# The first three batches' key DMAs: issued by GpSimd instead of SyncE

## The chip, the core and the metric

The kernel runs on one core of a Trainium2 chip. A core has TensorE (PE in the profile: matrix products into PSUM), VectorE (DVE), ScalarE (ACT), GpSimd (POOL) and SyncE (SP), which share a memory of 128 partitions and meet each other through semaphores. Each engine takes its own list of instructions in order. Transfers are asked for by an engine ("issued") and carried out by 16 DMA engines that the queues share; a semaphore is raised when a transfer has landed. The metric is the device time of one execution in microseconds.

## The reference

For 32 batches of 128 tokens by 128 features the reference chains four layers, each behind a layer norm and with a residual: cross attention A (16 heads of 8), a small mixture of experts, cross attention B (16 heads of 8, with an additive bias), and a large gated product of 8 heads by 8 experts (called C in the kernel).

```python
x = x + _L0_xattn_ref(_layernorm(x), ctx_1024, ctx_1024, mask_BxS2_if1, ...)   # A
x = x + _L0_ffn_ref(_layernorm(x), Ws1, Ws2, W1, W2, Wr)
x = x + _L1_xattn_ref(_layernorm(x), ctx_1024, mask_Bx1xSxS2_ff0, wq, wk, wv, wo)   # B
x = x + _L1_ffn_ref(_layernorm(x), q_w, k_w, v_w, o_w, sel_v_w, sel_o_w, route_scale)   # C

# inside A: keys, scores, and two masks (causal, and one row of 128 per batch)
scores = jnp.einsum('bhqd,bhkd->bhqk', q, k) * scale
full_mask = causal[None, None] & (mask[:, None, None, :] > 0)
scores = jnp.where(full_mask, scores, -jnp.inf)
p = jax.nn.softmax(scores, axis=-1)
```

## The kernel before, in words

One batch is worked on whole, in the stages A (with its experts), B and C, and the batches are pipelined: while C of one batch runs, B of a later and A of a still later one are interleaved with it. There is no scheduler. For each engine a list is written out by hand: `start()` for the prologue (batches 0 to about 6, some 145 us), `period(i)` for the middle and `end()`. Each call in a list, such as `a_queries(1)`, waits for its semaphores and then does its step for that batch; everything behind it on the same engine waits too.

TensorE computes the scores of A for four heads at once. For this the keys stand in a block-diagonal tile, `bdA`: each group of 32 partitions holds the keys of one head group and zeros elsewhere. The projected keys (`Kc0`, in the profile `Kc`) lie compactly, so they are spread into `bdA` by four small DMAs (8 partitions by 4 by 128 bf16, 8 KB each). A fifth DMA puts the mask row `keyrow` into `bdA`, and four more spread the queries `Qc0` into `Qb`. A's scores of a batch (`a_scores(b, 0)` on TensorE) need all nine. There is one `bdA`, one `keyrow` and one `Kc0`, reused by every batch, so:

- the spreading of batch b waits until the second scores of batch b-1 are done (`a_s2`);
- GpSimd makes the next `keyrow` (`a_masks` on GpSimd, from the raw mask `mrow_i`) only when the transfer of the last one has landed (`s_kmA`);
- ScalarE writes the next `Kc0` only when the last one's spreading has landed (`s_bdA`);
- SyncE loads the next raw mask (`masks(b)`) only when GpSimd has made the `keyrow` before it (`a_mask`).

SyncE issues nearly every DMA, in the order of its own list: inputs, masks, biases, A's spreading, and for B the writing of keys to DRAM rows (`k_rows`), their reading back into `bdB`, and the queries' spreading `Qs`. Its `masks(3)` stands right ahead of `a_queries(1)`. ScalarE issues the 512 KB weight loads (`raw`) that ScalarE and VectorE cut into `Vh`, `Vl`, `Oh`, `Ol` during the prologue, in between the attention work. TensorE fills part of its idle time in the prologue with a fixed number of matmuls by the identity whose result nobody reads (`psC<-ident_b`).

In the profile every matmul that goes through the helper has line L327, every ScalarE activation L1373, every DMA that SyncE issues through `load` L3832; a DMA issue is shown on the engine's queue as SPq or ACTq.

Of the kernel before, what the change touches and what calls it, by code (L numbers as in the profile page):

```python
# [14 lines left out]
SLOT = 32  # L15
# [23 lines left out]
def along(ap2, n):  # L39
    return ap2.unsqueeze(2).to_broadcast([ap2.shape[0], ap2.shape[1], n])  # L40
# [14 lines left out]
def program(nc, x_in, ctx_in, mask_in, bias_in, Wq0, bq0, Wk0, bk0, Wv0, bv0, Wo0, bo0,  # L55
# [4 lines left out]
    NH, HD = wq1.shape[1], wq1.shape[2]  # L60
    NJ = P // SLOT
# [19 lines left out]
    with ExitStack() as ctx:  # L81
# [3 lines left out]
        def sems(names):  # L85
            return [ctx.enter_context(nc.semaphore(n)) for n in names.split()]
# [173 lines left out]
        s_in = sems("in0 in1")  # L260
        s_bias = sems("bias0 bias1")
        s_out = sems("out0 out1")
        s_mask, s_bdA, s_qA, s_kmA, s_bdB, s_qB, s_rows, s_noK = sems("mask bdA qA kmA bdB qB k_rows no_K")
        s_bk, s_bq, s_wk0, s_wq0, s_wv0, s_wo0, s_attn1, s_ffn0, s_switch, s_rs, s_qk = sems(
            "w_bk w_bq w_wk0 w_wq0 w_wv0 w_wo0 w_attn1 w_ffn0 w_switch w_rs w_qk")
        s_raw = sems("w_raw0 w_raw1")
# [19 lines left out]

        IDENT, MINUS_HALF, ONEHOT, HIDDEN, LATE_B, SLOTS1, EARLIER = 4, 5, 11, 16, 19, 20, 28

        NG, NS = 12, 7

        place = {}

# [20 lines left out]
        def _(eng):  # L313
# [70 lines left out]
            def a_scores(b, t):  # L384
                if b not in BATCHES:
                    return
                if t == 0:
                    pe.wait_ge(s_const, LATE_B)
                    pe.wait_ge(s_kmA, 16 * (b + 1))
                    pe.wait_ge(s_qA, 16 * NJ * (b + 1))  # L390
                    pe.wait_ge(a_qb, b + 1)
                    pe.wait_ge(a_x2, b)
                elif t == 1:
                    pe.wait_ge(a_vb, b + 1)
                    pe.wait_ge(a_hT, b)
                else:
                    pe.wait_ge(a_nm, 4 * b + t - 1)
                o = heads_of(psA[:, t % 2, :])
                pe.wait_ge(s_bdA, 64 * (b + 1))
                mm(o, Qb[:, t, :], bdA[:, t], True, False)  # L400
                mm(o[:, :, LATE:], ident_b[:], over_heads(late_b[:], NJ), False, True).then_inc(a_s, 1)

# [963 lines left out]
        def _(eng):  # L1366
# [67 lines left out]
            def a_keys(b):  # L1434
                if b not in BATCHES:
                    return
                act.wait_ge(a_k, b + 1)
                act.wait_ge(s_bdA, 64 * b)
                copy(Kc0[:], psA[:, 1, 0:P]).then_inc(a_kb, 1)

            def a_values(b):
# [1842 lines left out]
        def _(eng):  # L3284
# [84 lines left out]
            def a_masks(b):  # L3369
                if b not in BATCHES:  # L3370
                    return
                pool.wait_ge(s_mask, 16 * (b + 1))
                pool.wait_ge(s_kmA, 16 * b)
                G.tensor_scalar(keyrow[:], mrow_i[:], 0, MASKED, ALU.is_le, ALU.mult).then_inc(a_mask, 1)

            def a_keys(b):
                if b not in BATCHES:
                    return
                pool.wait_ge(a_kb, b + 1)
                pool.wait_ge(s_bkC, 1)  # L3380
                G.tensor_tensor(Kc0[:].unsqueeze(1), Kc0[:].unsqueeze(1), along(bkC[:], P), ALU.add).then_inc(a_ks, 1)

            def a_values(b):
                if b not in BATCHES:
# [76 lines left out]
            def start():  # L3461
                constants()
                a_root(0)
                a_keys(0)
                a_values(0)
                a_queries(0)
                a_masks(0)
                a_masks(1)
                more_constants()
                a_causal(0, 0)  # L3470
                a_causal(0, 1)
                a_causal(0, 2)
                a_causal(0, 3)
                a_root(1)
                zeros()
                a_keys(1)
                a_values(1)
                a_root2(0)
                a_queries(1)
                a_masks(2)  # L3480
                b_root(0)
                a_root(2)
                b_below(0, 2)
                b_below(0, 3)
                a_causal(1, 0)
                a_causal(1, 1)
                a_causal(1, 2)
                a_causal(1, 3)
                a_keys(2)
                a_root2(1)  # L3490
                a_values(2)
                a_queries(2)
                b_root(1)
                c_root(0)
                a_masks(3)
                b_below(1, 2)
                a_causal(2, 0)
                a_causal(2, 1)
                a_causal(2, 2)
                a_causal(2, 3)  # L3500
                b_below(1, 3)
                a_root(3)
                a_keys(3)
                a_root2(2)
                a_values(3)
                a_queries(3)
                c_root(1)
                b_root(2)
                c_gates(0, 0)
                c_gates(0, 1)  # L3510
                c_gates(0, 2)
                a_causal(3, 0)
                a_causal(3, 1)
                b_below(2, 2)
                b_below(2, 3)
                values(0, 0, 0)
                a_causal(3, 2)
                a_causal(3, 3)
                values(0, 0, 1)
                values(0, 1, 0)  # L3520
                values(0, 1, 1)
                a_root(4)
                values(0, 2, 0)
                values(0, 2, 1)
                values(0, 3, 0)
                values(0, 3, 1)
                a_masks(4)
                a_keys(4)
                values(0, 4, 0)
                values(0, 4, 1)  # L3530
                values(0, 5, 0)
                values(0, 5, 1)
                a_root2(3)
                a_values(4)
                values(0, 6, 0)
                a_queries(4)
                values(0, 6, 1)
                values(0, 7, 0)
                values(0, 7, 1)
# [288 lines left out]
        def _(eng):  # L3828
# [65 lines left out]


            def a_masks(b):
                if b not in BATCHES:
                    return
                sp.wait_ge(s_zero, 8)
                sp.wait_ge(a_mask, b + 1)  # L3900
                sp.wait_ge(a_s2, 4 * b)
                load(bdA[KROW:KROW + 1].rearrange("p t j s -> p (t j) s"), keyrow[:], s_kmA)
# [15 lines left out]
                load(bias_sb[:, b % 2], bias_in[b, 0], s_bias[b % 2])  # L3918

            def a_keys(b):  # L3920
                if b not in BATCHES:
                    return
                sp.wait_ge(s_zero, 8)
                sp.wait_ge(a_ks, b + 1)
                sp.wait_ge(a_s2, 4 * b)
                for j in range(NJ):
                    load(bdA[SLOT * j + ROW0:SLOT * j + ROW0 + HD, :, j, :], Kc0[SLOT * j:SLOT * (j + 1)], s_bdA)
# [40 lines left out]
            def start():  # L3968
                values0()
                out0()  # L3970
                weights_switch()
                loads1()
                inputs(0)
                keys0()
                queries0()
                masks(0)
                products2()
                products()
                inputs(1)
                a_queries(0)  # L3980
                a_keys(0)
                a_masks(0)
                masks(1)
                weights_ffn()
                b_keys(0, 0)
                masks(2)
                no_keys()
                a_masks(1)
                inputs(2)
                b_keys(0, 1)  # L3990
                bias(0)
                masks(3)
                a_queries(1)
                a_keys(1)
                bias(1)
                b_queries(0)
                a_masks(2)
                inputs(3)
                a_keys(2)
                b_keys(1, 0)  # L4000
                a_queries(2)
                b_keys(1, 1)
                b_queries(1)
                bias(2)
                bias(3)
                a_masks(3)
                inputs(4)
                a_keys(3)
                b_keys(2, 0)
                a_queries(3)  # L4010
                masks(4)
                b_keys(2, 1)
                b_queries(2)
                masks(5)
                a_keys(4)
                a_queries(4)
                a_masks(4)
                b_keys(3, 0)
                bias(4)
                b_keys(3, 1)  # L4020
                b_queries(3)
                inputs(5)
                a_masks(5)
                inputs(6)
                a_queries(5)
                b_keys(4, 0)
                masks(6)
                a_keys(5)
                store(0)
                b_keys(4, 1)  # L4030
                b_queries(4)
# [64 lines left out]
```

## Time and profile before

| | us |
|---|---|
| median of 3 runs | 1418.85 (1418.19 to 1422.15) |
| the profiled execution | 1420.08 |
| its span, first to last instruction | 1418.3 |
| PE busy | 1368.3 (96%) |
| DVE busy | 1284.7 (91%) |
| ACT busy | 1217.4 (86%) |
| POOL busy | 920.9 (65%) |

The busy share of an engine is a mean over the whole span. The prologue is another regime: in the first 3 of the page's 40 slices (35 us each) PE is busy for 6, 6 and 7 tenths, and from the fifth to the last but one for 9 tenths or more. DMA issues are not counted as busy. The chain of waits, followed back from the last instruction, is on PE for 85% of the span and on SyncE's queue (SPq) for 3%.

### The profile page before, as it was taken

The page shows a single profiled execution, that of the slowest core. Times are in us where ns is not written, and L with a number is a line of the kernel's source. Part 1 is how long each engine was busy: PE and PEld are TensorE (multiplying, and loading weights), DVE is VectorE, ACT ScalarE, POOL GpSimd, SP SyncE. Part 2 cuts the span into 40 slices and gives each one's busy share as a digit, 9 for nine tenths or more (in the row PEclk, how much of TensorE's full clock was granted, in tenths as well). Part 3 has the DMA queues.
Part 4 walks back from the last instruction along what each step waited for, and adds up shares of the span by engine and source line. Part 5 has one row for each costly group of instructions (what it writes and reads, how often), then busy time and mean ns, then how long its engine had stood idle before and what let it go on. Part 6 is the DMA issues. An engine that isn't in the chain of part 4 may idle for free.

```text
span 1418.3 us, 34471 instructions
## 1 busy us (share of the span) xinstructions
PE 1368.3 (96%) x9554; PEld 922.0 (65%) x9711; DVE 1284.7 (91%) x5266; ACT 1217.4 (86%) x4234; POOL 920.9 (65%) x1409
## 2 busy tenths in 40 slices
PE   6678999999999999999999999999999999999997
PEld 3356666666666666666666666666666676666664
DVE  3679999999999999999999999999999999999986
ACT  3568888899988889998888999888899988889886
POOL 3224666667667666766766676676667666766777
PEclk9999999999999999999999999999999999999999
DMA  5520001100111110011111001111100111100000
GB/s 140 163 78 23 27 28 30 30 17 17 28 29 30 30 29 13 20 28 29 30 29 29 16 18 28 29 29 30 28 15 19 29 29 29 30 22 11 20 3 5
DMA packets 99968, 44.98 MB, mean 32 GB/s; under 512 B 21249, under 2 KB 99777, under 8 KB 99777
## 3 DMA queue, kind: packets, MB, share of 16 engines
q1 hardware_dynamic: 82560, 34.13, 8.7%
q10 hardware_dynamic: 17216, 8.65, 2.1%
q8 instruction: 78, 1.28, 0.4%
q14 instruction: 114, 0.93, 0.2%
HBM read 25.70 MB, written 8.52 MB: 24 GB/s over the span
## 4 chain that ended last, share of the span: by engine, by line
PE 85%; DVE 4%; POOL 3%; SPq 3%; issue 2%; ACT 2%; DMA 1%; POOLq 0%; ACTq 0%; DVEq 0%
PE psC L327 58%; PE psA L327 12%; PE psB L327 6%; PE psB L555 3%; SPq L3832 2%; PE psC L637 2%; DVE PTB L2398 1%; POOL accO L3445 1%; PE psA L489 1%; DVE nmA L2273 1%; POOL TE L3433 1%; PE psA L442 1%; DVE TE L2531 1%; ACT PTB L1373 1%; POOL v_sb L3438 1%
## 5 line engine op out<-in xcount | busy, mean ns | idle before, releaser
L1373 ACT ACTIVATE TE<-psC,gateO 128x128 f32<-128x128 f32 x1024 | 289.0, 378 | 30.5 <-PE psC L327 27.3
L2531 DVE SCALAR_TENSOR_TENSOR TE<-psC,gateO,TE 128x128 f32<-128x128 f32 x1024 | 286.9, 343 | 21.6 <-PE psC L327 11.8
L1373 ACT ACTIVATE TE<-psC,gate 128x128 f32<-128x128 f32 x1024 | 298.2, 400 | 7.2 <-PE psC L327 1.8
L2531 DVE SCALAR_TENSOR_TENSOR TE<-psC,gate,TE 128x128 f32<-128x128 f32 x1024 | 284.0, 340 | 7.3 <-PE psC L327 2.6
L3445 POOL TENSOR_TENSOR accO<-accO,TE 128x512 f32<-128x512 f32 x192 | 246.5, 1284 | 53.8 <-DVE TE L2531 44.6
L327 PE MATMUL psC<-Oh,ch 128*128 128x512 f32 x512 | 269.0, 525 | 0.0
L327 PE MATMUL psC<-Vh,xTh 128*128 128x512 f32 x512 | 263.1, 514 | 0.9 <-ACT PS L1373 0.9
L3433 POOL TENSOR_TENSOR TE<-TE 128x256 f32<-128x256 f32 x256 | 189.6, 741 | 56.3 <-DVE TE L2531 41.3
L327 PE MATMUL psC<-Oh,cl 128*128 128x512 f32 x512 | 202.1, 395 | 0.0
L327 PE MATMUL psC<-Vh,xTl 128*128 128x512 f32 x512 | 201.7, 394 | 0.0
L327 PE MATMUL psC<-Ol,cb 128*128 128x512 bf16 x477 | 185.8, 390 | 0.0
L327 PE MATMUL psC<-Vl,xTb 128*128 128x512 bf16 x393 | 153.4, 390 | 0.0
L327 PEld LDWEIGHTS psC<-Ol,cb 128*128 128x128 bf16 x512 | 49.0, 96 | 141.1 <-issue 141.1
L327 PEld LDWEIGHTS psC<-Vl,xTb 128*128 128x128 bf16 x512 | 49.2, 96 | 139.2 <-issue 139.2
L3438 POOL TENSOR_TENSOR v_sb<-TE 128x128 f32<-128x128 f32 x256 | 118.7, 464 | 13.7
L2398 DVE CUSTOM_DVE_ANT_0 PTB<-psB,bias_sb 128x128 f32<-128x128 f32 x512 | 114.9, 285 | 8.8 <-PE psB L327 6.4
L3360 POOL TENSOR_TENSOR PTB<-nmB,PTB 128x512 f32<-128x512 f32 x64 | 67.1, 1049 | 83.6 <-DVE nmB L2398 83.5
L1373 ACT ACTIVATE PTA<-psA 128x512 f32<-128x512 f32 x160 | 90.0, 614 | 23.3 <-PE psA L489 13.8
L327 PEld LDWEIGHTS psC<-Vh,xTh 128*128 128x128 f32 x512 | 99.4, 194 | 13.1 <-issue 6.5
L327 PEld LDWEIGHTS psC<-Oh,ch 128*128 128x128 f32 x512 | 99.9, 195 | 10.3
L327 PEld LDWEIGHTS psC<-Oh,cl 128*128 128x128 f32 x512 | 97.8, 191 | 5.9
L327 PEld LDWEIGHTS psC<-Vh,xTl 128*128 128x128 f32 x512 | 97.8, 191 | 4.8
(233 smaller groups left out, 3399.8 us busy)
## 6 DMA issues: line engine op xcount, KB each, us to landing
bdB<-k_rows SPq DMA_DIRECT2D x128, 64.0 KB, 2.2
k_rows<-Kc SPq DMA_DIRECT2D x96, 64.0 KB, 2.0
Qs<-Qc SPq DMA_DIRECT2D x96, 64.0 KB, 1.9
raw<-in_L_ffn_v_w ACTq DMA_DIRECT2D x8, 512.0 KB, 4.2
raw<-in_L_ffn_o_w ACTq DMA_DIRECT2D x8, 512.0 KB, 4.0
x_sb<-in_x SPq DMA_DIRECT2D x32, 64.0 KB, 2.0
ctx_sb<-in_ctx SPq DMA_DIRECT2D x32, 64.0 KB, 2.0
Qb<-Qc SPq DMA_DIRECT2D x128, 8.0 KB
```

Of the source, the lines that this page charges most:

```text
L327: return T.matmul(o, l, r, start=start, stop=stop)
L442: m = T.transpose(psA[:, 1, r * P:(r + 1) * P], UA[:, r * P:(r + 1) * P], ident)
L555: m = T.transpose(psB[:, t % 2, j * P:(j + 1) * P], PTB[:, t, j, :], ident)
L637: m = T.transpose(ps[:, j * P:(j + 1) * P], PS[:, 4 * i + j], ident)
L1373: return A.activation(o, i, func, **kw)
L2398: m = V.tensor_tensor_reduce(PTB[:, t, j], psB[:, t % 2, j * P:(j + 1) * P], bias_sb[:, b % 2], -1.0, LEAST, ALU.add, ALU.min, nmB[:, t, j ...
L2531: m = V.scalar_tensor_tensor(TE[:, i, e], psC[:, p, e * P:(e + 1) * P], gates[:, e:e + 1], TE[:, i, e], ALU.mult, ALU.add)
L3360: G.tensor_tensor(PTB[:, t], along(nmB[:, t, :], P), PTB[:, t], ALU.subtract).then_inc(b_sub, 1)
L3433: G.tensor_tensor(TE[:, i, 0:2], TE[:, i, 0:2], TE[:, i, 2:4], ALU.add).then_inc(v_fe, 1)
L3438: G.tensor_tensor(v_sb[:, h], TE[:, i, 0], TE[:, i, 1], ALU.add).then_inc(v_fe, 1)
L3445: G.tensor_tensor(accO[:], TE[:, slot(b, H1)] if h == 1 else accO[:], TE[:, slot(b, H1 + h)], ALU.add).then_inc(o_fe, 1)
L3832: SY.dma_start(dst, src).then_inc(s, 16)
```

## The change

For batches 0, 1 and 2 the five DMAs that spread the keys and the mask row into `bdA` leave SyncE's list and enter GpSimd's, behind `a_masks(0)`, `a_queries(1)` and `a_queries(2)`. They have semaphores of their own (`s_bdA0`, `s_kmA0`), and everyone who waited for the old ones waits for the new ones up to the third batch. Keys and mask row are now issued together, the four key DMAs first. From batch 3 on SyncE issues as before. No computing instruction is added or taken away.

```diff
+        EARLY = 3
+        def keys_spread(n):
+            return (s_bdA0, 64 * n) if n <= EARLY else (s_bdA, 64 * (n - EARLY))
+        def key_masks(n):
+            return (s_kmA0, 16 * n) if n <= EARLY else (s_kmA, 16 * (n - EARLY))
...
@@ tensor: a_scores
-                    pe.wait_ge(s_kmA, 16 * (b + 1))
+                    pe.wait_ge(*key_masks(b + 1))
-                pe.wait_ge(s_bdA, 64 * (b + 1))
+                pe.wait_ge(*keys_spread(b + 1))
...
@@ gpsimd: a_masks
-                pool.wait_ge(s_kmA, 16 * b)
+                if b:
+                    pool.wait_ge(*key_masks(b))
...
@@ gpsimd
+            def a_spread(b):
+                pool.wait_ge(s_zero, 8)
+                pool.wait_ge(a_ks, b + 1)
+                pool.wait_ge(a_mask, b + 1)
+                pool.wait_ge(a_s2, 4 * b)
+                for j in range(NJ):
+                    G.dma_start(bdA[SLOT * j + ROW0:SLOT * j + ROW0 + HD, :, j, :],
+                                Kc0[SLOT * j:SLOT * (j + 1)]).then_inc(s_bdA0, 16)
+                G.dma_start(bdA[KROW:KROW + 1].rearrange("p t j s -> p (t j) s"), keyrow[:]).then_inc(s_kmA0, 16)
...
@@ gpsimd: start
                 a_masks(0)
+                a_spread(0)
                 a_masks(1)
...
                 a_queries(1)
+                a_spread(1)
                 a_masks(2)
                 b_root(0)
...
                 a_queries(2)
+                a_spread(2)
                 b_root(1)
...
@@ sync: a_masks, a_keys
-                if b not in BATCHES:
+                if b not in BATCHES or b < EARLY:
...
@@ sync: start (the calls for batches 0 to 2 are gone)
                 a_queries(0)
-                a_keys(0)
-                a_masks(0)
                 masks(1)
...
                 a_queries(1)
-                a_keys(1)
                 bias(1)
```

GpSimd's list before, from the queries of batch 1 to the stages of B and A behind them. `Qc` and `Kc` are the compact queries and keys, `rsB` and `rsA` the layer norms' roots.

```order
L3396 TENSOR_TENSOR Qc<-Qc,bqC 128x128 [waits a_qb]
L3374 TENSOR_SCALAR keyrow<-mrow_i 16x128 [waits kmA,mask]
L3335 TENSOR_TENSOR rsB<-rsB,minus_half 128x1 [waits b_ln]
L3335 TENSOR_TENSOR rsA<-rsA,minus_half 128x1 [waits a_ln]
L3360 TENSOR_TENSOR PTB<-nmB,PTB 128x512 [waits b_nm] x2
```

The same place in the changed kernel:

```order
L3416 TENSOR_TENSOR Qc<-Qc,bqC 128x128 [waits a_qb]
L3399 DMA bdA<-Kc 8x4x128 [waits a_s2,a_mask,a_ks]
L3399 DMA bdA<-Kc 8x4x128 x3
L3401 DMA bdA<-keyrow 1x16x128
L3384 TENSOR_SCALAR keyrow<-mrow_i 16x128 [waits kmA_pool,mask]
L3344 TENSOR_TENSOR rsB<-rsB,minus_half 128x1 [waits b_ln]
L3344 TENSOR_TENSOR rsA<-rsA,minus_half 128x1 [waits a_ln]
```

The five DMAs now stand between the queries and the next mask row, and that mask row waits (`kmA_pool`) for the fifth of them to land.

SyncE's list before, at the same time in the program: the raw mask of batch 3, the queries and keys of batch 1, then the bias and B's queries of batch 0.

```order
L3832 DMA bias_sb<-in_mask_Bx1xSxS_ff 128x128
L3832 DMA mrow_i<-in_mask_BxS_if 16x128 [waits a_mask]
L3832 DMA Qb<-Qc 8x4x128 [waits a_q2,a_s,a_qs]
L3832 DMA Qb<-Qc 8x4x128 x3
L3832 DMA bdA<-Kc 8x4x128 [waits a_ks]
L3832 DMA bdA<-Kc 8x4x128 x3
L3832 DMA bias_sb<-in_mask_Bx1xSxS_ff 128x128
L3832 DMA Qs<-Qc 32x4x128 [waits b_qh,const]
```

In the changed kernel:

```order
L3855 DMA bias_sb<-in_mask_Bx1xSxS_ff 128x128
L3855 DMA mrow_i<-in_mask_BxS_if 16x128 [waits a_mask]
L3855 DMA Qb<-Qc 8x4x128 [waits a_q2,a_s,a_qs]
L3855 DMA Qb<-Qc 8x4x128 x3
L3855 DMA bias_sb<-in_mask_Bx1xSxS_ff 128x128
L3855 DMA Qs<-Qc 32x4x128 [waits b_qh,const]
```

The keys are gone from this place. The raw mask with its wait for `a_mask` (the mask row that GpSimd makes) still stands ahead of the queries.

## Rows read from the trace of the kernel before

**Rows 1.** Busy by stretch: stretch, us; PE, PEld, DVE, ACT, POOL; PEclk, DMA, GB/s.

```profile
20.70:22.80 2.10, 0.01 (x1) 0.13 (x2) 0.00 (x0) 0.57 (x2) 0.00 (x0) 1.00 0.67 164
...
43.00:48.70 5.70, 4.82 (x26) 2.65 (x25) 3.80 (x12) 3.25 (x7) 0.78 (x2) 1.00 0.58 162
48.70:50.80 2.10, 0.02 (x1) 0.13 (x2) 0.91 (x3) 1.00 (x2) 0.46 (x1) 1.00 0.57 159
...
123.00:200.00 77.00, 76.16 (x534) 51.43 (x541) 71.18 (x290) 68.09 (x244) 51.73 (x80) 1.00 0.09 26
```

**Rows 2.** The chain of waits, 0 to 60 us: start, us, what.

```profile
19.25 3.30 DMA bdA<-keyrow
...
22.86 0.25 PE psA L327
...
41.95 0.65 POOL keyrow L3374
...
42.62 0.33 SPq L3832
...
48.14 2.31 DMA bdA<-Kc
...
50.80 0.25 PE psA L327
...
55.97 0.86 PE psC L327 x4
```

**Rows 3.** Timeline of GpSimd: start, us, engine line op out<-in [idle before <-releaser].

```profile
13.20 1.03 POOL L3374 TENSOR_SCALAR keyrow<-mrow_i 16x128 bf16<-16x128 int32 x1
...
41.24 0.63 POOL L3396 TENSOR_TENSOR Qc<-Qc,bqC 128x128 bf16<-128x128 bf16 x1 [1.65 <-ACT Qc L1373]
...
77.84 0.87 POOL L3396 TENSOR_TENSOR Qc<-Qc,bqC 128x128 bf16<-128x128 bf16 x1 [0.67 <-ACT Qc L1373]
84.37 0.55 POOL L3335 TENSOR_TENSOR rsB<-rsB,minus_half 128x1 f32<-128x1 f32 x1 [5.66 <-DVE rsB L2250]
```

**Rows 4.** Timeline of SyncE's DMA issues.

```profile
9.46 1.29 SPq L3832 DMA_DIRECT2D x_sb<-in_x  x1
...
43.06 2.89 SPq L3832 DMA_DIRECT2D Qb<-Qc  x4
45.99 2.81 SPq L3832 DMA_DIRECT2D bdA<-Kc  x4
...
76.25 2.92 SPq L3832 DMA_DIRECT2D bdA<-Kc  x4
...
81.61 2.91 SPq L3832 DMA_DIRECT2D Qb<-Qc  x4
```

**Rows 5.** All that touches bdA, 0 to 125 us: durations min/median/max in ns.

```profile
L3832 SPq DMA_DIRECT2D bdA<-Kc x16: 665/672/750, 16.4 to 106.6; - x16
...
L3832 SPq DMA_DIRECT2D bdA<-keyrow x4: 578/589/597, 19.2 to 96.5; - x4
...
DMA to landing us min/median/max: 1.7/3.1/4.1
```

**Rows 6.** Timeline of all engines: fillers, the clearing of bdA, two adds of one shape.

```profile
8.17 1.06 PE L327 MATMUL psC<-ident_b 128*128 128x512 bf16 x2
...
10.69 0.43 POOL L3389 TENSOR_TENSOR Vb<-Vb,bvb 128x128 bf16<-128x128 bf16 x1 [0.47 <-ACT Vb L1373]
...
13.41 0.69 DVE L2220 COPY bdA<-hides 128x2048 bf16<-128x2048 bf16 x1
...
16.02 4.70 PE L327 MATMUL psC<-ident_b 128*128 128x512 bf16 x21
...
35.16 0.23 DVE L2313 TENSOR_TENSOR ob<-obA,bob 128x128 bf16<-128x128 bf16 x1
```

**Rows 7.** The chain of waits, 56 to 90 us.

```profile
83.84 1.84 DMA Qb<-Qc
```

**Rows 8.** Who waited for whom in 0 to 125 us: us, times, longest.

```profile
ACT Vh L1373 <- DMA raw<-in_L_ffn_v_w: 7.8, 5, 2.7
```

More of the change, by code:

```diff
@@ L262, in program @@
         s_out = sems("out0 out1")
-        s_mask, s_bdA, s_qA, s_kmA, s_bdB, s_qB, s_rows, s_noK = sems("mask bdA qA kmA bdB qB k_rows no_K")
+        s_mask, s_bdA, s_qA, s_kmA, s_bdB, s_qB, s_rows, s_noK, s_bdA0, s_kmA0 = sems(
+            "mask bdA qA kmA bdB qB k_rows no_K bdA_pool kmA_pool")
         s_bk, s_bq, s_wk0, s_wq0, s_wv0, s_wo0, s_attn1, s_ffn0, s_switch, s_rs, s_qk = sems(
@@ L1437, in a_keys @@
                 act.wait_ge(a_k, b + 1)
-                act.wait_ge(s_bdA, 64 * b)
+                if b:
+                    act.wait_ge(*keys_spread(b))
                 copy(Kc0[:], psA[:, 1, 0:P]).then_inc(a_kb, 1)
@@ L3372, in a_masks @@
                 pool.wait_ge(s_mask, 16 * (b + 1))
-                pool.wait_ge(s_kmA, 16 * b)
+                if b:
+                    pool.wait_ge(*key_masks(b))
                 G.tensor_scalar(keyrow[:], mrow_i[:], 0, MASKED, ALU.is_le, ALU.mult).then_inc(a_mask, 1)
@@ L3920, in a_keys @@
             def a_keys(b):
-                if b not in BATCHES:
+                if b not in BATCHES or b < EARLY:
                     return
@@ L3987, in start @@
                 no_keys()
-                a_masks(1)
                 inputs(2)
@@ L3993, in start @@
                 a_queries(1)
-                a_keys(1)
                 bias(1)
                 b_queries(0)
-                a_masks(2)
                 inputs(3)
-                a_keys(2)
                 b_keys(1, 0)
```

## The prediction

> **What bounds the kernel now.** I read the busy time by stretch first. From 123 us on TensorE is busy 76.16 of 77 us [rows 1]: the middle is bound by TensorE, and this change adds and takes nothing there. So only the prologue can move, and what it gains or loses is handed on as one shift of everything behind it. The two stretches before the scores of batches 0 and 1 show TensorE idle for about 2.1 us each (0.01 and 0.02 us busy, [rows 1]). The chain of waits then names the last thing awaited. Batch 0: the mask row's DMA, issued at 19.25, landed 3.30 later, and the scores start at 22.86 [rows 2]. Batch 1: GpSimd's mask row at 41.95, SyncE's raw-mask load at 42.62, the eight issues from 43.06, the last key DMA at 48.14 landing 2.31 later, scores at 50.80 [rows 2, 4]. Batch 2: the last query DMA at 83.84, landing 1.84 later at 85.68 [rows 7]. So SyncE's queue does stand on the path in all three batches, and the question is what GpSimd's costs there.
>
> **The price of an issue on GpSimd.** No row shows one. SyncE needs 0.67 us for a key DMA and 0.59 for the mask row [rows 5]; the longest issue of SyncE that I see is 1.29 us [rows 4]. For an add of one shape (128x128 bf16) GpSimd takes 0.43 us and VectorE 0.23 [rows 6], so it is the slow engine for small work. I take 1.05 us, some 1.5 times SyncE's 0.70 spacing (2.81 over four, [rows 4]), nearer to the upper end since descriptors for 32 scattered pieces are small work of that kind. It is an estimate; the ends 0.59 and 1.29 go into the range. A lower price than SyncE's I exclude only by judgement. Five issues are 5.25 us (2.95 to 6.45). For the landing behind the end of an issue I take SyncE's: 3.30 - 0.59 = 2.71 in batch 0, 2.31 - 0.67 = 1.64 in batches 1 and 2 [rows 2, 5].
>
> The Trainium skill (DMA: Bandwidth & Descriptors, Specifications) gives about 1 us to the first byte for a DMA issued by GpSimd and 0.6 for one by SyncE. That would add 0.4 to each landing, and by its rule the sum below would be some 1.2 us higher (three landings). No run here shows it yet.
>
> **Batch 0.** GpSimd's mask row ends at 14.23 [rows 3], the clearing of bdA at 14.10 [rows 6], so the issues start at about 14.25, 2.1 us ahead of SyncE's (16.40). They end at 19.50, and the mask row lands at 22.21 instead of 22.55. Gain 0.34 us. By the quick end they land at 19.9, but then TensorE's 21 fillers, which end at 20.72 [rows 6], stand ahead of the scores: the gain stops at 2.1. By the slow end they land at 23.41: a loss of 0.86. The keys' and mask's departure from SyncE also pulls the raw mask of batch 1 and the expert weights 3.4 us ahead, of which nobody on the path has need.
>
> **Batch 1.** Here the change adds a loop that the trace of before lacks. GpSimd's queries end at 41.87 [rows 3] and the DMAs follow at 41.95. Behind them stands the mask row of batch 2, which waits for the fifth one's landing. Behind that mask row, on SyncE, stands the raw-mask load of batch 3 (it waits for a_mask), and behind this, on the same queue, the queries of batch 1. Before, mask row, raw mask and queries followed within 1.1 us (41.95 to 43.06). Now the mask row starts at 41.95 + 5.25 + 1.64 + 0.08 = 48.92, 6.97 late, and the queries' four DMAs go out from 50.03. The fourth starts 2.22 behind the first and lands 2.31 later, at 54.56, and with the same 0.35 to the start the scores begin at 54.9 instead of 50.80. The 2.86 us in which SyncE formerly issued the keys behind the queries are already taken off in this. Loss 4.1 us (quick end: 2.95 + 1.1 + 0.08 - 2.86 = 1.3, with the shortest landing, 1.7 from issue [rows 5]; slow end 5.3). Also GpSimd's roots for B and A, the first computing behind, come later, but B's transpose stands behind A's scores on TensorE and moves with them. What SyncE holds behind the queries (bias, B's query spreading) moves by the same.
>
> **Batch 2.** Queries end on GpSimd at 78.71 [rows 3], issues 78.79 to 84.04, landing 85.68, which is when the queries landed before. On SyncE four issues (76.25, 2.92 us, [rows 4]) go from ahead of k_rows, so the queries go out about 1.0 us earlier and stop being last. GpSimd is free at 84.04, ahead of B's root at 84.37 [rows 3]. Sum 0 (quick end -1.0, when the queries are last again; slow end +1.2).
>
> **TensorE's pace.** Its idle stretch ahead of batch 1's scores grows from 2.1 to about 6.2 us. The granted clock reads 1.00, the 2.4 GHz level, in every stretch [rows 1], yet the first fillers took 0.53 us each (8.17) and later ones 0.22 (16.02) [rows 6]: after idleness the engine works at less than half pace for a while. On the chain behind it 0.25 us of scores and 0.86 of fillers are TensorE's [rows 2]; at 2.4 times that they take 1.5 us more. I take 0.6, as if it came about in four of ten cases.
>
> **Sum.** -0.34 + 4.1 + 0 + 0.6 = +4.4 us on the profiled execution's 1420.08. That execution was 1.2 above the median of the runs; the shift does not depend on this, so the forecast is 1418.85 + 4.4 = 1423.2, 0.31% more. A change of 0.3% (4.3 us) is about what a measurement of this kernel can tell from none, so it lies at that border.
>
> **Rivals.**
>
> *GpSimd issues as fast as SyncE.* At 0.67 each (3.35), batch 0 gains the full 2.1, batch 1 loses 3.35 + 1.64 + 0.08 - 2.86 = 2.2, batch 2 gains 1.0: -0.9, time 1418. For it: the work per DMA is the same. Against: the adds above. With 0.59 each and landings of 1.1 it is -1.8, time 1417. The sign turns at about 0.8 us per issue; below that the kernel is not slower. Chance 0.24.
>
> *GpSimd's issues are held up.* VectorE is busy 3.80 of the 5.70 us in which they would go out for batch 1 [rows 1], with weight cutting. If each issue stretches to 1.29, it is 0.9 + 5.3 + 1.2 + 0.6 = +8.0, time 1427. For it: GpSimd's own small operations stretch in the busy stretches, the queries' add from 0.63 to 0.87 us and the mask row to 1.03 [rows 3]. Against: batch 0's issues fall where VectorE does little. Chance 0.22. The Trainium skill (SBUF — State Buffer, Who interferes with whom) says that GpSimd cannot write descriptors while VectorE runs an operation in a two-port mode, and that such a DMA took 3.1 us instead of 0.62; by its figure this rival would be the larger one. What stands in that stretch is mostly adds and subtractions of two inputs, which the page does not count among those modes.
>
> *The delay is absorbed.* ScalarE waits 7.8 us for weight loads in the prologue [rows 8]; if weights are what is late behind 51 us, a delay of A's scores costs only part. Of 4.1 about 3 would vanish, time 1420. Against: the weight cutting stands behind A's row maxima in VectorE's list and moves with them. Chance 0.10.
>
> *No loop, since the landing is seen early or the mask row is early enough.* That would need the landing wait not to bind; the wait list of the changed order names it, so I give it 0.04, at about 1417.
>
> **How the numbers follow.** The forecast has 0.40 and falls on both sides of the border, 0.27 above and 0.13 within. Rival one: 0.20 within, 0.04 faster. Rival two is slower, 0.22. Absorbed: within, 0.10. No loop: within 0.02, faster 0.02. So slower 0.49, same 0.45, faster 0.06. The range takes rival one's 1418 nearly whole and rival two's 1427: 1417.5 to 1427.5.
>
> **What would show it.** Five issues on POOLq at about 14.3, 42 and 79 us; their mean is the first test (1.05). The start of A's scores: 22.5, 54.6 and 90 or so (from 22.86, 50.80 and about 86). GpSimd's mask row of batch 2 at about 48.6, waiting for the DMA of the key row, then raw mask and queries on SyncE right behind. After 123 us all else shifted by one amount. I would be wrong if the issues take under 0.8 us, if SyncE's queries of batch 1 go out near 43, or if the shift at 123 us differs from that at batch 2's scores.

## Result

The changed kernel takes 1423.86 us (median of 14 runs), the one before 1420.32 in the same comparison; the ratio is 1.0025, 95% interval 1.0018 to 1.0032. That is 3.5 us slower where 4.4 were forecast (on a base of 1418.85, the median of the first three of these 14 runs of before).

The profiled execution alone would mislead. It took 1420.88, the fastest of the 14, and its span of 1419.1 is only 0.8 above the 1418.3 of before. Single executions of the unchanged kernel lie between 1417.4 and 1424.2 (94 of them, run beside the experiments). So the times below are ratios with their intervals, and the profiles are read for what follows what.

GpSimd's timeline in the changed kernel (start, us, engine line op), answering to [rows 3]:

```profile
14.55 2.44 POOL L3399 DMA_DIRECT2D bdA<-Kc  x4 [0.86 <-DVE bdA L2229]
16.98 0.53 POOL L3401 DMA_DIRECT2D bdA<-keyrow  x1
21.80 0.64 POOL L3384 TENSOR_SCALAR keyrow<-mrow_i 16x128 bf16<-16x128 int32 x1 [4.29 <-DMA bdA<-keyrow]
...
39.63 0.63 POOL L3416 TENSOR_TENSOR Qc<-Qc,bqC 128x128 bf16<-128x128 bf16 x1 [1.30 <-ACT Qc L1381]
40.25 2.30 POOL L3399 DMA_DIRECT2D bdA<-Kc  x4
42.54 0.53 POOL L3401 DMA_DIRECT2D bdA<-keyrow  x1
46.19 0.66 POOL L3384 TENSOR_SCALAR keyrow<-mrow_i 16x128 bf16<-16x128 int32 x1 [3.12 <-DMA bdA<-keyrow]
46.93 0.57 POOL L3344 TENSOR_TENSOR rsB<-rsB,minus_half 128x1 f32<-128x1 f32 x1
```

Batch 1's five DMAs are issued within 2.8 us (40.25 to 43.07), then the next mask row waits 3.12 us for the last of them to land. SyncE's issues, answering to [rows 4]:

```profile
46.88 0.33 SPq L3855 DMA_DIRECT2D mrow_i<-in_mask_BxS_if  x1
47.32 2.91 SPq L3855 DMA_DIRECT2D Qb<-Qc  x4
```

Raw mask and queries stand right behind that mask row, as the loop has it: 7.7 us from GpSimd's queries (39.63) to SyncE's (47.32), where before it took 1.8 [rows 3, 4]. TensorE (timeline), with the last fillers and the scores of batch 1:

```profile
45.00 2.11 PE L335 MATMUL psC<-ident_b 128*128 128x512 bf16 x9
52.81 0.35 PE L335 MATMUL psA<-late_b,ident_b 128*128 128x176 bf16 x1 [5.71 <-issue]
52.96 0.42 PE L531 MATMUL psB<-ident_r,xnB 128*128 128x128 f32 x1
```

It idles for 5.71 us instead of 2.1, and the first matmul that is recorded behind it takes 0.35 us instead of 0.24. The busy time by stretch (stretch, us; PE, PEld, DVE, ACT, POOL; PEclk, DMA, GB/s), answering to [rows 1], shows why:

```profile
50.00:52.80 2.80, 0.00 (x0) 0.14 (x2) 0.00 (x0) 0.00 (x0) 0.00 (x0) 0.90 0.62 181
52.80:54.00 1.20, 1.19 (x5) 0.70 (x5) 0.80 (x2) 0.28 (x1) 0.00 (x0) 0.50 0.00 0
54.00:55.00 1.00, 1.00 (x5) 0.66 (x6) 1.00 (x2) 0.28 (x1) 0.00 (x0) 0.50 0.00 0
```

The granted clock (PEclk) is 0.50, the 1.2 GHz level, for the first 2 us behind the idle stretch. In the kernel before it read 1.00 there.

What one DMA costs on either queue (durations min/median/max in ns), answering to [rows 5]:

```profile
L3399 POOL DMA_DIRECT2D bdA<-Kc x12: 547/548/807, 14.6 to 82.6; - x12
L3855 SPq DMA_DIRECT2D bdA<-Kc x4: 672/677/751, 106.2 to 108.4; - x4
L3401 POOL DMA_DIRECT2D bdA<-keyrow x3: 530/530/530, 17.0 to 83.1; - x3
```

GpSimd issues faster than SyncE, 0.55 against 0.67 us. The profile lists its DMAs as a queue of another kind (packets, MB, share of the 16 engines):

```profile
q0 software_dynamic: 480, 0.11, 0.0%
```

And who held SyncE's queue in the first 125 us (us, times, longest). Before, the mask row held it for 2.3 us in all, once:

```profile
SPq L3855 <- POOL keyrow L3384: 8.4, 2, 7.5
```

### The profile page after: what moved, and what is told of

It reads as the page before. It is cut to its first block, busy times and chain, and to the rows that moved or that the text cites. A ratio compares the mean times of both kernels' runs of the same rounds, so it can differ in the third digit from the quotient of the medians.

```text
span 1419.1 us, 34473 instructions
## 1 busy us (share of the span) xinstructions
PE 1370.1 (97%) x9554; PEld 922.9 (65%) x9711; DVE 1285.3 (91%) x5266; ACT 1219.2 (86%) x4234; POOL 930.6 (66%) x1424
## 4 chain that ended last, share of the span: by engine, by line
PE 87%; DVE 4%; POOL 3%; issue 2%; ACT 2%; SPq 1%; DMA 1%; POOLq 0%; ACTq 0%; DVEq 0%
PE psC L335 59%; PE psA L335 13%; PE psB L335 6%; PE psB L563 3%; PE psC L645 2%; DVE PTB L2407 1%; POOL accO L3465 1%; PE psA L497 1%; DVE nmA L2282 1%; POOL TE L3453 1%; PE psA L450 1%; SPq L3855 1%; DVE TE L2540 1%; ACT PTB L1381 1%; POOL v_sb L3458 1%
```

## The experiments

Each ratio is to the kernel before, run on the same chip in the same comparison (14 runs of the changed kernel, 6 of e1, 11 of each other); medians of different rows come from different comparisons, so rows are compared by their ratios. The fourth column is the time in us from GpSimd's queries of batch 1 (`Qc`) to the first matmul by `late_b` in batch 1's scores on TensorE, in the kernel's one profile: it leaves out what happened earlier in that execution. (The record of the matmul ahead of that one, `psA<-bdA,Qb`, is missing in most profiles, so this one serves as the mark.) The last is the mean over the runs of each run's mean granted clock.

| kernel | median us | ratio (95%) | Qc to scores | clock |
|---|---|---|---|---|
| before | 1420.53 (94 runs) | 1 | 9.56 | 0.9971 |
| changed | 1423.86 | 1.0025 (1.0018, 1.0032) | 13.18 | 0.9949 |
| e1 more fillers | 1423.34 | 1.0028 (1.0016, 1.0039) | 12.86 | 0.9972 |
| e2 queries first | 1419.33 | 0.9996 (0.9986, 1.0005) | 7.54 | 0.9960 |
| e3 mask row first | 1419.74 | 1.0000 (0.9990, 1.0009) | 9.37 | 0.9965 |
| e4 fewer fillers, before | 1420.97 | 1.0009 (1.0000, 1.0018) | 9.68 | 0.9954 |
| e5 roots first | 1420.59 | 1.0004 (0.9995, 1.0013) | 7.55 | 0.9958 |
| e6 batch 0 only | 1420.39 | 1.0000 (0.9991, 1.0009) | 9.58 | 0.9973 |
| e7 batch 1 only | 1422.80 | 1.0017 (1.0009, 1.0026) | 13.07 | 0.9963 |
| e8 queries first, before | 1421.18 | 1.0008 (0.9999, 1.0017) | 9.12 | 0.9965 |
| e9 two mask rows | 1420.52 | 0.9997 (0.9987, 1.0007) | 9.44 | 0.9970 |
| e10 batch 2 only | 1420.36 | 0.9994 (0.9985, 1.0003) | 9.74 | 0.9971 |
| e11 all three | 1419.37 | 0.9988 (0.9979, 0.9997) | 7.54 | 0.9976 |
| e12 fillers batch 0, before | 1421.36 | 1.0004 (0.9995, 1.0013) | 9.72 | 0.9970 |

**e1, more fillers.** Changed kernel, TensorE's list:

```diff
-                warm(9)
+                warm(29)
                 a_scores(1, 0)
```

> The changed kernel with 29 instead of 9 filler matmuls ahead of the scores of batch 1, so that TensorE's idle stretch there (5.71 us in the changed kernel's trace) shrinks to about 1.4. Pace theory (the idle stretch lowers TensorE's clock, and in most runs for longer than in the profiled one): the scores start at 52.8 as before, the granted clock reads 1.00 in 52.8 to 56, the mean clock of the runs returns from 0.994 to 0.999, and the time falls by 2 to 3 us, to about 1421. Loop theory alone (the late start is all there is, the clock costs nothing): the time stays at 1423.9 within 0.7.

Measured 1.0028. The timeline and the stretches:

```profile
47.61 6.42 PE L335 MATMUL psC<-ident_b 128*128 128x512 bf16 x29
55.10 0.24 PE L335 MATMUL psA<-late_b,ident_b 128*128 128x176 bf16 x1 [1.06 <-issue]
```

```profile
52.80:54.00 1.20, 1.20 (x6) 0.39 (x4) 0.00 (x0) 0.00 (x0) 0.00 (x0) 1.00 0.90 256
54.00:56.00 2.00, 0.86 (x6) 0.59 (x7) 0.63 (x2) 0.28 (x1) 0.00 (x0) 1.00 0.12 33
```

The idle stretch and the fall of the clock are gone (1.00 in both stretches, mean clock from 0.9949 to 0.9972), the time is not better. (In this execution batch 0's scores had started 1.0 us later than in the changed kernel's profile, and Qc was 2.6 later, so the absolute start says nothing; from Qc it is 12.86 against 13.18.) The pace theory (the idle stretch lowers TensorE's clock, and that is what costs) falls as an account of the loss: the clock did fall, and giving it back brought nothing that these runs can tell. By the two intervals taken together, a gain of up to some 2 us is not excluded.

**e4, fewer fillers.** The kernel before with `warm(9)` at this place taken out.

> The kernel before, without the 9 filler matmuls ahead of the scores of batch 1: nothing is later, but TensorE idles about 4.2 us there instead of 2.1. Pace theory: the granted clock falls below 1.00 at 50.8 to 53 in some or all runs, mean clock 0.995 to 0.997, time 1 to 3 us more than before. Loop theory alone: same time as before within 0.7 us.

Measured 1.0009 (1.0000 to 1.0018). The other side of e1, the stretches:

```profile
50.00:52.80 2.80, 1.93 (x7) 1.25 (x9) 1.54 (x3) 1.37 (x4) 0.00 (x0) 0.62 0.73 207
52.80:54.00 1.20, 1.20 (x4) 0.30 (x3) 1.20 (x4) 0.47 (x2) 0.00 (x0) 0.50 0.00 1
```

TensorE idles 4.14 us there, and the clock falls to the same level with nothing else changed. The one profile would not show that the longer idleness did it: in the profile of e12 the clock fell at the same place behind 2.25 us of idleness, about as long as in the kernel before, whose profile reads 1.00. What speaks for it is the mean clock, 0.9954 against 0.9968 of the kernel before in the same comparison. The version costs 0 to 2.6 us, 1.3 by the middle. So the price of a fall is at the edge of what these runs can tell, and e1 shows that it is not what made the changed kernel slow.

**e2, queries first.** Changed kernel, SyncE's list:

```diff
-                masks(3)
                 a_queries(1)
+                masks(3)
                 bias(1)
```

> The changed kernel with SyncE's raw-mask load of batch 3 moved behind the query DMAs of batch 1. Loop theory: the queries go out at 40.3 instead of 47.3, the scores then wait for the mask row (landing 46.1) and for the fillers (ending 47.1), and start at about 47.1 instead of 52.8; with the clock kept the time is 1423.9 - 5.7 - 2 = about 1416, under both kernels. Rival (GpSimd's slow landings are the price, whatever the order on SyncE): the scores start no earlier than 51 and the time stays at or above 1422.

Measured 0.9996, that is 4.1 us under the changed kernel by the ratios (4.5 by the medians): the loss is gone, with every GpSimd DMA still in place. GpSimd, SyncE and TensorE in its timelines:

```profile
40.03 0.63 POOL L3416 TENSOR_TENSOR Qc<-Qc,bqC 128x128 bf16<-128x128 bf16 x1 [1.39 <-ACT Qc L1381]
...
47.02 1.17 POOL L3384 TENSOR_SCALAR keyrow<-mrow_i 16x128 bf16<-16x128 int32 x1 [3.56 <-DMA bdA<-keyrow]
48.26 0.57 POOL L3344 TENSOR_TENSOR rsB<-rsB,minus_half 128x1 f32<-128x1 f32 x1
```

```profile
40.69 2.90 SPq L3855 DMA_DIRECT2D Qb<-Qc  x4
48.21 0.34 SPq L3855 DMA_DIRECT2D mrow_i<-in_mask_BxS_if  x1
```

```profile
47.57 0.24 PE L335 MATMUL psA<-late_b,ident_b 128*128 128x176 bf16 x1
49.27 0.33 PE L531 MATMUL psB<-ident_r,xnB 128*128 128x128 f32 x1 [1.46 <-DVE xnB L2262]
```

The queries go out at once and the scores start about as forecast (47.57 for 47.1), but the time falls by 4.1 to 4.5 and not by 7.7. From Qc the scores start 2.0 us earlier than in the kernel before, and the time is the same: B's transpose behind the first scores waits until 49.27 for batch 0's normalised input, whose root (48.26) stands behind the mask row on GpSimd. From Qc the transpose is at 9.24 us, where before it was at 9.64, so nearly all that the scores gained ends in the next wait.

**e5, roots first.** As e2, and on GpSimd:

```diff
                 a_spread(1)
-                a_masks(2)
                 b_root(0)
                 a_root(2)
+                a_masks(2)
```

> As the kernel with the queries first, and on GpSimd the roots of B (batch 0) and A (batch 2) now stand ahead of the next mask row, so that they do not wait for the landing of the mask row's DMA either. There the second matmul of the group waited until 49.27 us for B's normalised input. Loop theory (everything that stood behind the landing is what costs): root of B at about 46 instead of 48.2, B's transpose at about 47.8, all later work 1.5 us earlier than there: median 1417.5 to 1418, 2.5 to 3 under the kernel before. Rival (latency of GpSimd's DMAs itself, or the clock, decides now): 1419.3 as with the queries first.

Measured 1.0004; a miss. In its profile B's transpose starts 8.87 us behind Qc, against 9.24 in e2, a gain of 0.4 and not 1.5. GpSimd's root (48.39) waits for VectorE, which waits for the experts of batch 0 on TensorE, and behind the root a weight cut of 1.3 us on VectorE (48.93) still stands ahead of the normalised input (50.18); that chain is what is late next.

**e3, mask row first.** Changed kernel, GpSimd issues the mask row's DMA ahead of the four key DMAs.

```diff
+                G.dma_start(bdA[KROW:KROW + 1]..., keyrow[:]).then_inc(s_kmA0, 16)
                 for j in range(NJ):
                     G.dma_start(bdA[...], Kc0[...]).then_inc(s_bdA0, 16)
-                G.dma_start(bdA[KROW:KROW + 1]..., keyrow[:]).then_inc(s_kmA0, 16)
```

> The changed kernel with the mask row's DMA issued ahead of the four key DMAs on GpSimd. The loop then closes four issues (2.3 us) earlier. Loop theory: the next mask row on GpSimd starts at about 44 instead of 46.2, scores of batch 1 at 50.6 instead of 52.8, idle 3.5 us; time 1421.5, and if the clock does not fall at this idle length about 1419.5. Rival (the four key DMAs' landing decides, or landing counts from the last issue whatever the order): no change, 1423.9.

Measured 1.0000 (1419.74, next to the second of the two numbers, 1419.5). GpSimd and SyncE:

```profile
41.05 0.63 POOL L3398 DMA_DIRECT2D bdA<-keyrow  x1
41.67 2.18 POOL L3400 DMA_DIRECT2D bdA<-Kc  x4
43.94 0.89 POOL L3384 TENSOR_SCALAR keyrow<-mrow_i 16x128 bf16<-16x128 int32 x1
```

```profile
45.30 2.92 SPq L3855 DMA_DIRECT2D Qb<-Qc  x4
```

The landing now passes while the four key DMAs are issued, and the mask row waits for nothing: it starts 2.3 us behind the end of its DMA's issue, where it was 3.1. From Qc (40.47) the queries go out after 4.8 us instead of 7.7, and the loss is gone.

**e9, two mask rows.** Changed kernel, both orders as they are:

```diff
-        keyrow = sb("keyrow", [NH, P], BF16)
+        keyrow = sb("keyrow", [NH, 2, P], BF16)
...
-                if b:
-                    pool.wait_ge(*key_masks(b))
-                G.tensor_scalar(keyrow[:], mrow_i[:], ...)
+                if b > 1:
+                    pool.wait_ge(*key_masks(b - 1))
+                G.tensor_scalar(keyrow[:, b % 2], mrow_i[:], ...)
```

> The changed kernel, orders untouched, with two buffers for the mask row, so that GpSimd's next mask row waits for no landing. GpSimd's DMAs stay where they are. Loop theory (the wait for the landing, with what stands behind it, is the loss): from GpSimd's queries of batch 1 to the scores of batch 1 it takes at most 9.5 us (13.2 in the changed kernel, 9.6 in the one before), and the time falls by 3 to 4 us to about 1420. Rival (GpSimd's slow landing of keys and mask row holds the scores itself, so the wait only hid it): 12 us or more, and 1423.

Measured 0.9997. This takes away GpSimd's wait for the landing, and nothing else:

```profile
42.43 2.29 POOL L3399 DMA_DIRECT2D bdA<-Kc  x4
44.72 0.53 POOL L3401 DMA_DIRECT2D bdA<-keyrow  x1
45.32 0.86 POOL L3384 TENSOR_SCALAR keyrow<-mrow_i 16x128 bf16<-16x128 int32 x1
```

```profile
46.22 0.33 SPq L3855 DMA_DIRECT2D mrow_i<-in_mask_BxS_if  x1
46.66 2.93 SPq L3855 DMA_DIRECT2D Qb<-Qc  x4
```

The mask row follows the issues without a wait, and from Qc to the scores it is 9.44 us, as before the change. With e2 and e3 this settles the cause: three different cuts of the same loop each bring the time back to that of the kernel before. In all three the idle stretch and the fall of the clock go with the loop; that the clock alone is not the cause rests on e1.

**e6, e7, e10, one batch at a time.** `EARLY` becomes a set ({0}, {1} or {2}), with the semaphore counts by membership and SyncE's calls for the other two back at their places.

> Only batch 0's five DMAs on GpSimd, those of batches 1 and 2 on SyncE at their old places. Loop theory: the part of the change that gains. Scores of batch 0 at 21.9 (before 22.86), GpSimd's queries of batch 1 at about 40.6 (41.24), scores of batch 1 at 49.8 (50.80); time 1 us under the kernel before, 1419.4. Rival (the three parts work alike): a third of the loss, 1421.5.

> Only batch 1's five DMAs on GpSimd. Loop theory: this part holds the whole loss. GpSimd's DMAs at 41.9 to 44.7, its next mask row at 47.9, queries out on SyncE at about 49.0, scores at 54.3 instead of 50.8; time 3.5 us above the kernel before, plus about 1 for a lower mean clock: 1424 to 1425. Rival (the three parts work alike): 1421.5.

> Only batch 2's five DMAs on GpSimd. Both theories: next to nothing; from GpSimd's queries of batch 2 to its scores 7.8 us instead of 8.15, time 0.3 us under the kernel before, same within 0.7. If it is slower by more than 1 us, the root of B behind the issues is a second loss that the loop theory lacks.

Measured 1.0000, 1.0017 and 0.9994, each to about 0.0009: batch 1 is the only part that is clear of no change. The three add up to 1.6 us of the 3.5; the other 1.9 are not assigned and are within what these intervals leave open. The kernel of e7:

```profile
45.33 0.53 POOL L3405 DMA_DIRECT2D bdA<-keyrow  x1
48.79 1.19 POOL L3386 TENSOR_SCALAR keyrow<-mrow_i 16x128 bf16<-16x128 int32 x1 [2.93 <-DMA bdA<-keyrow]
```

```profile
50.44 2.91 SPq L3859 DMA_DIRECT2D Qb<-Qc  x4
```

The same loop, 13.07 us from Qc to the scores; its 2.4 us by the ratio are under the 3.5 to 4.5 forecast. Batch 0's part, expected to gain 1 us, shows no gain (between 1.3 us less and 1.3 us more). Batch 2's part was to bring its scores to 7.8 us behind Qc from 8.15; its profile has 8.26. In the kernel of e6:

```profile
17.44 0.53 POOL L3405 DMA_DIRECT2D bdA<-keyrow  x1
23.87 0.64 POOL L3386 TENSOR_SCALAR keyrow<-mrow_i 16x128 bf16<-16x128 int32 x1 [5.90 <-DMA bdA<-keyrow]
```

The wait for the landing took 5.90 us here, 4.29 in the changed kernel's profile. Batch 0's scores start between 21.93 and 24.17 us in the profiles in which GpSimd issued all five of its DMAs, and between 22.54 and 23.00 where SyncE did: the head start of about 2 us on the queue is used up by a later and less regular landing. The change itself has a hand in what else moves then: with the keys gone from SyncE's list, the expert weights (`W1s` and `W2s`, 256 KB each) are issued at 17.18 and 18.86 instead of 20.95 and 22.66, right beside the mask row's DMA, and the DMA engines' busy share is 1.00 from 17 to 22 us. That these loads lengthen the landing is a reading; no run took them away.

**e8, queries first in the kernel before.** The move of e2, without GpSimd's DMAs.

> The kernel before, with SyncE's raw-mask load of batch 3 behind queries and keys of batch 1 instead of ahead. It tells how much of the gain of the reordered changed kernels needs GpSimd's DMAs. The mask row on GpSimd costs 1.06 us of the queries' way there (41.95 to 43.06), so loop theory gives scores at 49.8 instead of 50.80 and 1419.4; that is 1.5 to 2 above the kernel with roots first. Rival (this order alone gives all of the gain): 1418 or less.

Measured 1.0008, no gain where 1 us was expected: the queries go out 1.2 us earlier from Qc, but the keys behind them land last, and from Qc to the scores it is 9.12 instead of 9.56, too little to see. So the order by itself does not bring e2's 4 us; those need the landing in the loop.

**e11, all three.** The changed kernel with e2's order, e9's two buffers and `warm(26)` instead of `warm(21)` ahead of batch 0's scores.

> The changed kernel with the queries first on SyncE, two mask-row buffers, and 26 instead of 21 fillers ahead of the scores of batch 0 (which reach to about 21.8 us, into the idle stretch after which the clock fell to 1.2 GHz in some profiles). Loop theory: scores of batch 1 start 6 to 7.5 us behind GpSimd's queries, and B's transpose with them, time 1417.5, 3 us under the kernel before. Rival (time off the prologue is given back before the middle, or to the clock): 1419.5 or more.

Measured 0.9988 (0.9979 to 0.9997): 1.7 us under the kernel before, the one version whose interval excludes no change on the fast side, and short of the 3 expected. VectorE and TensorE:

```profile
46.55 0.29 DVE L2371 TENSOR_TENSOR x<-psA,x 128x128 f32<-128x128 f32 x1 [0.94 <-PE psA L335]
...
48.18 1.29 DVE L2248 TENSOR_TENSOR Vl<-raw,Vh 128x512 bf16<-128x512 f32 x2 [0.60 <-ACT Vh L1381]
49.39 0.34 DVE L2262 TENSOR_SCALAR xnB<-x,mvB,rsB 128x128 f32<-128x128 f32 x1
```

```profile
48.52 0.24 PE L335 MATMUL psA<-late_b,ident_b 128*128 128x176 bf16 x1
49.78 0.33 PE L531 MATMUL psB<-ident_r,xnB 128*128 128x128 f32 x1 [1.03 <-DVE xnB L2262]
```

The scores are early, and then TensorE waits for what comes behind batch 0's experts: x at 46.55, its root on GpSimd at 47.66, a weight cut on VectorE at 48.18, and the normalised input at 49.39. B's transpose is 8.80 us behind Qc, where before it was 9.64: of 2.0 us that the scores gained, 0.8 go on. Which of the three edits brings the 1.7 us is not shown; the first two alone gave 0.9996 (e2) and 0.9997 (e9).

**e12, fillers of batch 0 in the kernel before.** `warm(29)` instead of `warm(21)`.

> The kernel before with 29 instead of 21 fillers ahead of the scores of batch 0, which closes TensorE's idle stretch of 2.1 us at 20.7 to 22.8. Pace theory (part of the scatter of all kernels comes from the clock falling behind that stretch): the granted clock stays 1.00 in 24 to 28, mean clock of the runs up by 0.001, time 0.6 to 1 us less than before, and less scatter. Rival: no difference.

Measured 1.0004; the rival was right. The mean clock stayed (0.9970 against 0.9972 in the same comparison) and the time did not fall. In some profiles (e1, e6, e7, e8) the clock reads 0.57 to 0.60 in 24 to 28 us and Qc of batch 1 comes at 42.2 to 42.8, where it is at 39.6 to 41.8 in the profiles that read 1.00 there; filling the idle stretch ahead does not lower the median.

## Why the prediction was right

**The loop of batch 1** was the step that carried the sum, and it holds as it stood: GpSimd's DMAs, their landing, the next mask row, SyncE's raw mask, the queries, the scores. Forecast loss 4.1 us; from Qc to the scores the profiles have 3.6 (13.18 against 9.56), and by e7's ratio that batch's part is worth 2.4 of the 3.5 (1.3 to 3.7, by its interval).

**Luck in the number.** The two prices in that sum were wrong in opposite directions. An issue was put at 1.05 us and takes 0.55, below even the lower end of 0.59; the reasoning from a slow add on GpSimd to slow issuing does not hold. The landing was taken from SyncE's rows as 1.64 us and takes 3.1. Together the stretch from the first issue to the mask row was put at 6.97 us and took 5.94 (40.25 to 46.19). The rival of quick issues thus had the right price and the wrong sign: its turning point of 0.8 us per issue rested on SyncE's landing. With the measured issues and the landing left as it was, the prediction's own sum would have been -2.1 for batch 0, +1.7 for batch 1, -1.0 for batch 2 and 0.6 for the pace, together -0.8: faster, not slower. That the total came out near is owed to the longer landing, which the sum did not have. The Trainium skill (DMA: Bandwidth & Descriptors, Specifications) had the direction: by its 0.4 us more to the first byte the forecast landing would have been 2.0, as an estimate, against 3.1 here.

**By its own signs of being wrong** it did not come off clean. The issues took under 0.8 us, which was one of them, and the answer is the landing. The queries did not go out near 43, so the second did not come. The third, a shift at 123 us unlike that at batch 2's scores, did come in the pair of profiles: 1.84 us at batch 2's scores, but 0.90 at GpSimd's queries of batch 5 (start 183.03 before, 183.93 changed), and about as much to the end. So the delay was not handed on whole there.

**Batch 0**, forecast -0.34: nothing that e6 could tell (1.0000). In the changed kernel's one profile it looked like a gain of 0.93. Here too quick issues and a late landing cancel. **Batch 2**, forecast 0: 0.9994 in e10, its interval holding no change; the scores come 7.84 us behind Qc instead of 8.15 in the changed kernel's profile, but 8.26 in e10's, and 7.72 and 7.74 in those of e6 and e7, where SyncE issues this batch's DMAs. So no gain can be put down to GpSimd.

**TensorE's pace**, 0.6 as an allowance: the clock did fall (0.50 in 52.8 to 55). The prediction had this as a guess from the first fillers, 0.53 us each in a stretch whose granted clock read 1.00, which is not the same sign. Its price stays open between 0 and some 2 us: e4 has 1.3 by the middle for more idleness alone, e1 nothing for its removal. Over the 94 runs of the kernel before, a mean clock lower by 0.001 goes with 0.60 us more, and the changed kernel's clock is lower by 0.0022; that is a correlation, and e1 speaks against reading 1.3 us of cause into it.

**Held-up issues** (VectorE in the way of GpSimd): four key DMAs took 2.44, 2.30 and 2.31 us in the three batches, with VectorE busy for 0.50 us of the first stretch and for 1.6 of either other. The 0.14 more in the first is the first DMA of GpSimd's queue, which took 0.81 us, and it did so too where the queue's first was batch 1's (e7) or batch 2's (e10). No issue came near the 1.29 of this rival, but the quick issues were mostly over before the weight cutting that it had in mind (42.78) began. Of what the Trainium skill says here (SBUF — State Buffer, Who interferes with whom) no run is a test: VectorE's longer operations beside the issues (0.69 us and more) had two inputs or read PSUM, and those of the kinds that it names for a two-port mode were of 0.29 us at most. **Absorbed**: not by batch 2, whose scores still have it (87.83 against 85.99). Behind that the profiles disagree: from GpSimd's queries of batch 2 to those of batch 5 the shift falls from 2.15 to 0.90 us in the changed kernel's and from 4.44 to 3.93 in e7's, and grows from 4.19 to 5.21 in e1's. Each is a single execution, so whether a part is regularly absorbed stays open.

## What to carry to other kernels

When a DMA moves to another engine's queue, look less at the price of the issue than at who waits for the landing and what stands in order behind that waiter, on every queue it feeds. Here the next batch's mask row, needed by nobody soon, held the raw mask of the batch after it, and through SyncE's order the queries that were needed at once; a second 4 KB buffer or two exchanged lines take the loss away. And one profile of a kernel whose runs scatter by 0.3% can show a quarter of the true difference.

## What the runs showed of the hardware that was not expected

- GpSimd issues a small DMA (32 pieces of 256 bytes) in 0.55 us, SyncE in 0.67. The first one of GpSimd's queue took 0.81.
- From the end of the mask row's issue on GpSimd to the instruction that waits for it: 4.3 us in batch 0 and 3.1 in batch 1 of the changed kernel, 3.6 in e2, 2.9 in e7, 5.9 in batch 0 of e6; SyncE's in batch 0 took 2.7 [rows 2, 5]. In e3, where the mask row's DMA went first, it had landed within 2.3. The DMA engines' busy share was 1.00 in 17 to 22 us and 0.69 in 43 to 46.2 (changed), with weight loads of 256 and 512 KB; which part of the landing is the queue's own and which those loads' was not tried.
- TensorE's granted clock fell to the 1.2 GHz level behind idle stretches of 5.71 us (changed) and 4.14 us (e4). Behind shorter ones it fell only in some executions: before batch 0's scores behind 1.4 to 2.8 us (e1, e6, e7, e8), while it read 1.00 behind 2.1 to 2.6 us there in others (before, e5, e9), and before batch 1's scores behind 2.25 us in e12.
